# First expert stage with a fixed DRAM region per expert, one tile list after routing, and residual, sum and norm done on the expert tiles

## The reference, cut to what matters

```python
h = h + L2_attn(layernorm(h))   # one head; the diagonal of the scores is masked out
# first experts: top 1 of 8, no capacity limit
x = layernorm(h); route = sigmoid(x @ Wr + br)
e = argmax(route); prob = max(route)
h = h + prob * (gelu(x @ W1[e]) @ W2[e])        # W1 256x1024, W2 1024x256
h = h + L3_attn(layernorm(h))   # 16 heads, causal, with a slope per head
h = h + L3_ffn(layernorm(h))    # second experts, each with a fixed capacity of 333 rows
```

## Time and profile before

| what | us |
|---|---|
| median of 3 runs | 2289.98 (2289.2 to 2295.62) |
| the profiled execution, whole | 2287.08 |
| its span, first to last instruction | 2285.3 |
| PE busy | 1807.9 (79%) |
| DVE busy | 1140.6 (50%) |
| ACT busy | 759.1 (33%) |
| POOL busy | 502.2 (22%) |
| TensorE clock granted, mean | 0.920 of full |

### The profile page before, as it was taken

The page is one execution under the profiler, slowest core; times in us unless marked ns, Lnnn a source line. Parts: engine busy times, 40 slices in busy tenths (PEclk is TensorE's granted clock), DMA queues, the critical chain, the costliest instruction groups (busy, mean ns, idle before and its releaser), DMA issues. The chain is left out here.

```text
span 2285.3 us, 32329 instructions
## 1 busy us (share of the span) xinstructions
PE 1807.9 (79%) x9490; PEld 1178.8 (52%) x9490; DVE 1140.6 (50%) x3699; ACT 759.1 (33%) x1873; POOL 502.2 (22%) x728
## 2 busy tenths in 40 slices
PE   0049999998897989777763999768888888882998
PEld 0024444444665667554541677535666555661676
DVE  5346767673326766744552222156665666641111
ACT  0004444453231245221210221137555566630211
POOL 0130100001101122301111111114434444531122
PEclk9999999998997999899885999859998999995999
DMA  8444544444200000160000101030000010002332
GB/s 179 133 79 89 106 81 87 72 72 121 84 18 0 1 1 1 39 257 12 12 13 24 33 30 33 26 106 9 16 17 19 24 25 19 19 19 59 129 135 70
DMA packets 72299, 129.65 MB, mean 57 GB/s; under 512 B 23030, under 2 KB 59573, under 8 KB 67442
## 3 DMA queue, kind: packets, MB, share of 16 engines
q1 hardware_dynamic: 52636, 107.80, 18.1%
q0 software_dynamic: 17632, 14.26, 2.5%
q10 hardware_dynamic: 1893, 5.99, 0.8%
HBM read 89.79 MB, written 39.52 MB: 57 GB/s over the span
## 5 line engine op out<-in xcount | busy, mean ns | idle before, releaser
L2304 POOL TENSOR_SCALAR l_P<-l_P,l_ri 111x111 f32<-111x111 f32 (+1 forms) x256 | 178.3, 714 | 159.3 <-DVE l_ri L2492 158.4
L653 ACT ACTIVATE PT<-psT 111x666 f32<-111x666 f32 x192 | 139.4, 726 | 156.4 <-PE psT L734 156.0
L2586 ACT ACTIVATE l_P<-l_S,l_nm 111x111 f32<-111x111 f32 (+2 forms) x384 | 179.3, 471 | 32.7 <-DVE l_nm L2485 32.5
L554 DVE TENSOR_REDUCE mx<-psS 111x2 f32<-111x666 f32 x192 | 159.6, 847 | 25.7 <-PE psS L719 25.7
L745 PE MATMUL psO<-PT,vS 111*32 111x333 f32 x768 | 147.0, 461 | 0.1
L2706 PE MATMUL l_psP<-ident,l_P 111*111 111x111 f32 x768 | 108.8, 281 | 32.2 <-DVE l_PT L2501 27.6
L2706 PEld LDWEIGHTS l_psP<-ident,l_P 111*111 111x111 f32 x768 | 95.4, 189 | 62.9 <-issue 33.1
L2042 DVE COPY t_hT<-t_psG 128x512 f32<-128x512 f32 x56 | 36.1, 686 | 175.0 <-PE t_psG L2085 175.0
L2485 DVE CUSTOM_DVE_ANT_0 l_S<-l_psA,l_am 111x111 f32<-111x111 f32 (+1 forms) x256 | 79.0, 331 | 76.9 <-PE l_psA L2692 70.1
L2074 PE MATMUL t_psH<-expert_w,t_xT 128*128 x224 | 103.4, 606 | 1.5 <-DVE t_xT L2035 1.2
L2097 PE MATMUL t_psY<-expert_w,t_hT 128*128 x448 | 101.4, 379 | 0.6 <-ACT t_yb L2007 0.6
(11 more groups left out here) (401 smaller groups left out, 3744.4 us busy)
## 6 DMA issues: line engine op xcount, KB each, us to landing
expert_w<-in_moe_dram SPq DMA_DIRECT2D x8, 2048.0 KB, 24.6
c_w<-in_moe_dram SPq DMA_DIRECT2D x16, 1024.0 KB, 7.2
qs<-halves_scratch SPq DMA_DIRECT2D x128, 83.5 KB, 3.2
ks<-halves_scratch SPq DMA_DIRECT2D x128, 83.5 KB, 4.1
halves_scratch<-high SPq DMA_DIRECT2D x32, 167.0 KB, 3.0
halves_scratch<-low SPq DMA_DIRECT2D x32, 167.0 KB, 3.6
c_xb<-xs_scratch SPq DMA_DIRECT2D x8, 667.3 KB
xs_scratch<-zeros SPq DMA_DIRECT2D x6, 777.0 KB
```

The costliest lines, as they stand in the source:

```text
L554: v.tensor_reduce(mx[J % 2][:, t, c:c + 65:64], psS[s % 2][0:TT, :, 0:T], AX.X, ALU.max, negate=True).then_inc(max_done, 1)
L653: s_.activation(PT[jp % 2][:, :, a, :], psT[0:TT, :, 0:T], ACT.Exp).then_inc(exp_done, 1)
L2304: r = g.tensor_scalar(Pt, Pt, ri[:, c % 2, 2 * t + half:2 * t + half + 1], None, ALU.mult)
L2586: s_.activation(P[c % 4][:, half, at(t):at(t + 1)], Sm[:, half, at(t):at(t + 1)], ACT.Exp, bias=nm[:, c % 2, i:i + 1], scale=-1.0, accum_o ...
```

## The change

It has five parts.

1. `xs` now has a region of 2688 rows for each of the 8 experts, so that a token's row is region start plus rank and `route_place` needs no allocation. `tiles()` builds the list of 28 tiles (their first row in `tile_row`, their expert in `tile_expert`) once, behind the last batch. The zero fill covers 21632 rows of 258 floats, and `xs2` as 2688 rows of 513 floats, all by DMAs of 128 partitions; it is waited for in `quantised`, a stage later.
2. In `masked_attention` the routed rows and slots have two buffers, the order of the pieces is `rl`, `v` 0, `v` 1, `v` 2, `rk`, and `norm(b + 2)` stands between `v` 2 and `rk` in place of `norm(b + 1)` between the first two rows of scores. The add of epsilon is moved to DVE, so POOL's part is one `pow` without a drain. Three whole bodies stand unrolled behind the loop, where there was one.
3. SP writes `h` of each batch to DRAM after attention.
4. In `top1_experts` POOL gathers the residual rows by token to `hb`. DVE multiplies the product by the row's probability (now a column of the row), adds the residual and computes mean and variance; POOL does the `pow`, and DVE writes the normalised row beside the sum. One scatter sends both (2 x 256 floats). ACT no longer copies the product. There are four input buffers, and a tile's load waits for the sum four tiles earlier.
5. `alibi_attention` loads the normalised rows straight to `xn` and all of `h` by one DMA, for which DVE waits ahead of the first scores. `take`, `scale_taken` and `norm` are gone.

```diff
+def stats_and_eps(nc, vector, sh, b):
+    batch_stats(nc, vector, sh, b)
+    return v.tensor_scalar(sh.var_eps[:, :], sh.batch_mv[:, :, 1], EPS, None, ALU.add)
+def eps_scale(nc, sh, b):
+    return nc.gpsimd.tensor_tensor(sh.rs[:, bass.ds(NT * b, NT)], sh.var_eps[:, :], sh.mhalf[0:TT, 0:NT], ALU.pow)
...
 class Fill: write
-            parts = 128 if f.shape[0] % 128 == 0 else TT
-            flat = f.rearrange("(p r) c -> p (r c)", p=parts)
+            flat = f.rearrange("(p r) c -> p (r c)", p=128)
...
 class Routed
-        self.xs = nc.dram_tensor("xs_scratch", [128 * MOE_TILES, ROW1], F32, kind="Internal").ap()
-        self.ys = nc.dram_tensor("ys_scratch", [B * T, D], F32, kind="Internal").ap()
+        self.tile_row = sb("tr", [TT, MOE_TILES], I32)
+        self.xs = dram("xs_scratch", E * REGION + 128, ROW1)
+        self.h = dram("h1_scratch", B * T, D)
+        self.ys = dram("ys_scratch", B * T, 2 * D)
...
 masked_attention, SP and POOL
+            def send(b):
+                sync.wait_ge(stats_done, b + 1)
+                sync.dma_start(routed.h[bass.ds(b * T, T), :].rearrange("(t p) c -> p t c", p=TT),
+                               sh.h[:, bass.ds(NT * b, NT), :]).then_inc(h_sent, 16)
...
             def scale(b):
-                pool.wait_ge(stats_done, b + 1)
+                pool.wait_ge(eps_done, b + 1)
                 pool.sem_inc(begun, 1)
-                batch_scale(nc, pool, sh, sc_tmp, b, "plain", scale_done)
+                eps_scale(nc, sh, b).then_inc(scale_done, 1)
...
 masked_attention, DVE, route_place: 20 instructions of the running allocation out
+                v.tensor_tensor(w[:, :, :], w[:, :, :], oh[:, :, :], ALU.mult)
+                dve.wait_ge(p_ready, b + 1)
+                v.tensor_scalar(pe_m[:, :], pe_m[:, :], 1.0, None, ALU.add)
+                dve.drain()
+                v.tensor_reduce(sl[:, :], w[:, :, :], AX.X, ALU.add)
+                v.reciprocal(row[p][:, :, D + 1], pe_m[:, :])
+                dve.drain()
+                v.tensor_copy(slot[p][:, :], sl[:, :]).then_inc(slot_ready, 1)
+            def tiles():                       # 15 instructions, once
...
                 row_max(0)
-                if not last:
-                    dve.wait_ge(piece_done, base(b))
-                    norm(b + 1)
                 row_max(1)
...
+                piece("rl", 0)
                 piece("v", 0)
-                piece("rl", 0)
                 combine(2)
                 piece("v", 1)
+                piece("v", 2)
+                if later(b):
+                    dve.wait_ge(piece_done, number("x", 1, b, first, last)[1] + 1)
+                    norm(b + 2)
                 piece("rk", 0)
-                piece("v", 2)
                 dve.drain()
-                batch_stats(nc, dve, sh, b).then_inc(stats_done, 1)
+                stats_and_eps(nc, dve, sh, b).then_inc(eps_done, 1)
+                dve.sem_inc(stats_done, 1)
...
 top1_experts, SP
-                if s >= 2:
-                    sync.wait_ge(x_turned, s - 1)
-                    sync.wait_ge(xT_ready, s - 1)
-                sync.dma_start(xb[s % 2][:, :], routed.xs[128 * s:128 * s + 128, :]).then_inc(x_in[s % 2], 16)
+                at = nc.sync.value_load(routed.tile_row[0:1, s:s + 1], min_val=0, max_val=E * REGION)
+                if s >= 4:
+                    sync.wait_ge(y_out, s - 3)
+                sync.dma_start(xb[s % 4][:, :], routed.xs[bass.ds(at, 128), :]).then_inc(x_in[s % 4], 16)
...
 top1_experts, POOL: fetch(s) gathers hb, scale(s) is the pow, send(s) scatters
+            for s in range(NS):
+                if s + 2 < NS:
+                    fetch(s + 2)
                 if s >= 2:
                     send(s - 2)
+                if s >= 1:
+                    scale(s - 1)
...
 top1_experts, DVE
+            def sums(s):
+                dve.wait_ge(y_done, s + 1)
+                dve.wait_ge(hb_in[s % 4], 16 * (s // 4 + 1))
+                if s >= 2:
+                    dve.wait_ge(y_sent[s % 2], 16 * (s // 2))
+                new = yb[s % 2][:, 0:D]
+                v.scalar_tensor_tensor(new, psY[:, 0:D], xb[s % 4][:, D + 1:D + 2], hb[s % 4][:, :], ALU.mult, ALU.add
+                                       ).then_inc(y_out, 1)
+                dve.drain()
+                v.bn_stats(mom[:, :], new)
+                dve.drain()
+                v.bn_aggr(mv[s % 2][:, :], mom[:, :])
+                dve.drain()
+                v.tensor_scalar(ve[s % 2][:, :], mv[s % 2][:, 1:2], EPS, None, ALU.add).then_inc(moments_ready, 1)
+            def rows(s):
+                dve.wait_ge(scaled, s + 1)
+                v.tensor_scalar(yb[s % 2][:, D:2 * D], yb[s % 2][:, 0:D], mv[s % 2][:, 0:1], rs[s % 2][:, 0:1],
+                                ALU.subtract, ALU.mult).then_inc(rows_ready, 1)
...
             for s in range(NS):
                 hidden_out(s)
                 if s + 2 < NS:
                     input_out(s + 2)
+                if s >= 2:
+                    rows(s - 2)
+                if s >= 1:
+                    sums(s - 1)
...
 alibi_attention, SP
-                sync.dma_start(xn[:, :, :], routed.ys[bass.ds(b * T, T), :].rearrange("(t p) c -> p t c", p=TT)
-                               ).then_inc(y_in, 16)
+                sync.dma_start(xn[:, :, :], routed.ys[bass.ds(b * T, T), D:2 * D].rearrange("(t p) c -> p t c", p=TT)
+                               ).then_inc(x_in, 16)
...
             sync.dma_start(br[:, :], ins["c_br"].partition_broadcast(TT)).then_inc(wr_in, 16)
+            sync.dma_start(sh.h[:, :, :], routed.ys[:, 0:D].rearrange("(n p) c -> p n c", p=TT)).then_inc(h_in, 16)
             fetch(1, 2)
             stream.prefetch(sync)
...
 alibi_attention, DVE: take, norm and their calls out; ahead of the first rows()
-            take(1)
+            dve.wait_ge(h_in, 16)
```

More of the change, by code:

```diff
@@ L1186, in dequantise, with quantised @@
         pool.drain()
-def quantised(nc, sh, pre):
+def quantised(nc, sh, pre, fill):
     NS = 3 * B
@@ L1216, in quantised, with _ @@
         tok = lambda banks, t: banks[t // 2][0:TT, D * (t % 2):D * (t % 2) + D]
+        @block.sync
+        def _(sync):
+            fill.wait(sync)
         @block.gpsimd
@@ L1462, in masked_attention @@
         bq = sb("bq", [128, KT])
-        sc_tmp = sb("tmp", [TT, 3, NT])
-        row = sb("row", [TT, NT, ROW1])
+        row = [sb(f"row{i}", [TT, NT, ROW1]) for i in range(2)]
         rT = sb("rT", [128, KT, T])
@@ L1505, in batches, with later @@
             body(0, 0, True, False)
-            with eng.Fori(0, (B - 2) // 2) as i:
+            with eng.Fori(0, (B - 4) // 2) as i:
                 body(2 * i + 1, 1, False, False)
                 body(2 * i + 2, 0, False, False)
-            body(B - 1, 1, False, True)
+            for b in range(B - 3, B):
+                body(b, b % 2, False, b == B - 1)
+        def later(b):
+            return not isinstance(b, int) or b + 2 < B
         def base(b):
@@ L1543, in _ @@
             experts.load(sync, ins["moe1"], range(E))
-            sync.wait_ge(scattered, 16 * NT * B)
+            def send(b):
+                sync.wait_ge(stats_done, b + 1)
+                sync.dma_start(routed.h[bass.ds(b * T, T), :].rearrange("(t p) c -> p t c", p=TT),
+                               sh.h[:, bass.ds(NT * b, NT), :]).then_inc(h_sent, 16)
+            batches(sync, lambda b, p, first, last: send(b))
+            sync.wait_ge(h_sent, 16 * B)
+            for p in range(2):
+                sync.wait_ge(scattered[p], 8 * NT * B)
         @block.gpsimd
@@ L1559, in _ @@
             g.memset(one8[:, :], 1.0)
[L1560 to L1564, removed]
+            for x in (before[:, 0, :], region[:, :]):
+                g.iota(x, pattern=[[REGION, E]], base=0, channel_multiplier=0, allow_small_or_imprecise_dtypes=True)
             pool.drain()
@@ L1690, in route_place @@
-                dve.drain()
-                v.tensor_tensor(past_all[:, :], past_all[:, :], past_now[:, :], ALU.add)
-                dve.drain()
+                v.tensor_copy(routed.tile_row[:, :], used[:, :])
+                v.tensor_copy(routed.tile_expert[:, :], expert[:, :])
             norm(0)
+            dve.wait_ge(piece_done, 2)
+            norm(1)
             for t in range(NT):
@@ L2123 @@
 CAP = B * T // E
+FILL2 = (E * CAP + 127) // 128 * 128
 ROW = 2 * D + 1
@@ L2520, in body @@
                 for c in range(NC):
-                    if c == 0 and not last:
-                        norm(b + 1)
                     if c + 1 < NC or not last:
@@ L2545, in body @@
                         route_rows(b - 1)
-                    if c == 6 and later(b):
-                        take(b + 2)
                 if last:
```

245 lines of the change are left out of this document (114 added, 131 removed).

## The result

The changed kernel takes 2229.99 us (median of 4 runs, 2226.2 to 2233.31), the kernel before 2292.38 in the same session (4 runs, 2289.2 to 2295.62). The ratio is 0.9727, 95% interval 0.9704 to 0.975. Forecast were 2226, range 2209 to 2248.

The account below looks back on a forecast made before the run. Masked attention was taken as bound by a chain crossing engines, neither PE nor DVE full. Terms -32 - 1 - 10 + 0.4 + 0 + 3.6 + 2 - 27 = -64 from 2287.1 gave 2223, with 2.9 for the median 2226; range 2209 to 2248.

Parts of the forecast that it names:

- masked loop, six ends: Masked attention, batch ends 1 to 6: shorter `route_place` and undrained `pow` gain 5.3 us each, -32 in all.
- masked tail, with the register load: End of masked attention: two shorter `route_place` and a `pow` without add and drain, -10; SP's register load from `tile_row`, +0.4.
- first experts, tiles: First experts, 26 tiles: new work and loads are on time, so a tile stays at 7.98 us, 0.
- first experts, the rest: End of first experts: sum, moments, `pow`, row and wakes replace a copy and one wake, +3.6 us.
- alibi head: Ahead of the first alibi scores: the load of `h`, on three engines at 73 GB/s, lands about F + 51 (F: fetch), +2.
- alibi loop: Alibi loop without `take` and `norm`: six times 4.3 us, priced from batch 6 as control, and 1.2 for `norm(1)`, -27.
- zero fill, unchanged stages: Zero fill beside the recurrence, grown from 9.2 to 27.8 MB: ends near 631, hidden, 0.
- P to slot: Masked loop, from `route_place`'s start (P) to the slot's start: from 4.33 to about 1.5 us.
- slot to `pow`: Masked loop, from slot to `pow` start: 9.76 us, of which 3.87 for add and drain goes.
- second rival: First experts held by tile loads or gathers, 0.5 to 0.9 on 26 tiles: +13 to +23, 2239 to 2249; chance 0.11.
- view of 16 engines: Alibi head: were 16 engines used for every DMA, the load of `h` would be fast and the sum 6 us lower.
- first rival: Masked attention: `pow` still waits for POOL's pending scatters, rows 3.9 later in six batches and the tail, 2253; chance 0.07.

Follow-up runs that it names:

- e9: Changed kernel with POOL's add and drain ahead of the `pow` back, and SP's store of `h` held until the next batch's first rows are added; 2265.29 us, one run.
- e2: Changed kernel with 17 small drained DVE instructions added to `route_place`, 11 ahead of the slot's copy and 6 behind; 2265.85 us, ratio 0.9894 to the kernel before.
- e3: Changed kernel with the old order of pieces in masked attention and `norm(b + 1)` again between the first two row maxima; 2229.21 us, ratio 0.9723 to the kernel before.
- c0: Changed kernel run once more, unchanged, as control; 2233.56 us, ratio 0.9741 to the kernel before.
- e5: Changed kernel with the load of `h` in the alibi head split into 96 and 15 partitions; 2231.61 us, ratio 0.974 to the kernel before.
- e7: Changed kernel with the alibi head's load of `h` split into 96 and 15 partitions and masked attention's `pow` ahead of the previous batch's scatters; 2216.25 us.
- e10: Changed kernel with the zero fill written by DMAs of 111 partitions in place of 128, the same 27.8 MB; 2411.73 us, one run.
- e1: Changed kernel with POOL's add of epsilon and the drain behind it put back ahead of the `pow` in masked attention; 2289.01 us, ratio 0.9986 to the kernel before.

## Why the prediction was right, step by step

| step | forecast | measured |
|---|---|---|
| masked loop, six ends | -32 | -35.3 |
| batch 0 and the stage's start | -1 | -1.3 |
| masked tail, with the register load | -9.6 | -8.0 |
| first experts, tiles | 0 | +0.4 |
| first experts, the rest | +3.6 | +4.7 |
| alibi head | +2 | +2.0 |
| alibi loop | -27 | -29.0 |
| zero fill, unchanged stages | 0 | +9.5 |

The forecast had the waits right, and most of their sizes. That the medians come within 4 us of it is in part luck: the loops gained 5.3 more than forecast, the tail and the experts gave 3.1 of that back, and two such executions differ by several us in stages that nothing touches.

**Masked loop.** The terms, from the first two rows of the table of periods: P to slot 2.87 (forecast 2.8), slot to `pow` 4.04 (3.87), given back ahead of P 1.05, the rest 0.1. Net 5.9 a batch for 5.3. The 1.05 is what the forecast's own terms give, 1.65 for `v` 2 and the norm less 0.6 for the norm that left the middle. Its terms sum to 5.6 (6.6 - 1.65 + 0.6), of which it took 5.3.

**What the sum didn't know.** It added the two gains as if each were worth its length. In the changed kernel each is worth more: the drain put back lengthens slot to `pow` by 4.0 and the period by 5.9 (e9), the long `route_place` lengthens P to slot by 2.7 and the period by 5.4 (e2). The surplus is PE's: it is idle for 5.01 and 3.76, its clock falls to half, and the parts of the period behind the rows grow by 1.6 and 2.7. In the kernel before the wait for the `pow` cost PE less, since its last work ahead of the rows ended 13.9 behind P; in e9 that is 8.5. Its rows, and the clock in this idle, still full:

```profile
1188.28 0.54 PE L1890 MATMUL m_psP<-ident,m_P 111*111 111x111 f32 x3 [0.38 <-ACT m_P L1804]
1191.23 0.48 PE L1849 MATMUL m_psM<-ident,m_row 111*128 111x111 f32 x3 [2.40 <-DVE m_row L1612]
```

```profile
1190.00:1191.00 1.00, 0.00 (x0) 0.00 (x0) 1.00 (x5) 0.00 (x0) 0.00 (x0) 1.00 0.00 0
```

Against the kernel before, e9 and e2 gain almost nothing (31.0 to 31.0 and to 30.5), and the changed kernel 5.9. But both have the new order too, which by e3 costs 1.06 ahead of P and gives it back only behind the `pow`. No run has the old order with one wait alone, or the new order with both, so how much of this is the two waits acting together and how much the order stays open. The total was right because both waits went in one change. I read the clock of the whole loop, 0.85, but didn't ask what a shorter wait would do to it.

**Tail.** From the first addition of the last batch to the last slot it is 10.3 shorter, as forecast. From there to the next stage's first load it is 2.3 longer: the stage ends 1.3 later behind its last scatter, and the register load takes 1.0, not 0.4. In c0 this tail took 3.5 more than in the profiled changed kernel, on PE products at half clock (six of them 2.77 there and 1.46 here); so its gain is 4.5 to 8.

**First experts.** The second rival, tile loads or gathers, didn't come: 7.98, with the slack foreseen (1.4, measured 1.25). The end was underestimated by 1: from the last product's end to the next stage 10.7 us against 6.1. The last scatter, twice as wide, is issued by 1442.3 and the stage ends 6.2 later; before it was 3.9. So the chain of sum, moments and row added 2.3 and not 3.6, and the end of the scatter another 2.3 that the forecast didn't have; what it waits for there, no run tells.

**Alibi head.** Three engines at 73 GB/s gave F + 51; it was F + 51.67. By a view of 16 engines the head would have been 6 shorter, and e5, which makes 16 of the 3, measures 4.1 (5.1 in e7). The speed that 16 engines then reach, 200 GB/s and not five times 73, no row of before had told. The Trainium skill, in the section "Why a DMA increments its semaphore by 16 and not by 1" of its page "DMA: Bandwidth & Descriptors", has a DMA of 96 partitions run on 16 engines, and by its rule (the largest number up to 16 that divides) one of 111 on 3. The shares in e5 (1.10), after (0.20) and e10 (0.19) agree.

**Alibi loop.** Batch 6 as a control gave 4.5 less the transpose, 4.3. From c = 6 to the next c = 0 the six batches gained 2.7 to 5.0, 26.1 in all (six times 4.3 is 25.8), and batch 6 nothing. The stage as a whole is less certain than its -29.0: in the ten other executions with this loop unchanged it took 525.4 to 536.8, against 532.75 in the profiled one.

**Zero fill.** The recurrence was 3.9 longer, which looked like its cost. It isn't a fixed one: in ten other executions with the large fill (all but e10) the stage took 169.9 to 174.7, and e2's, at 169.89 and a clock of 0.94, is shorter than the one of before (170.65). Where it took 174.7, the clock was 0.92. Whether the fill makes the lower clock likelier stays open, since only one profile of the kernel before exists. The fill can't be the whole of it: ahead of the recurrence, where the fill hasn't begun and nothing was changed, all twelve executions with the change took 548 to 559 against the 546.00 of that one profile, and the quantised stage took about 159.8 in five of the thirteen executions and 162.4 to 163.0 in the others. So the +9.5 is no term of the change that these runs show.

**The first rival** (the `pow` waits anyway) falls by the timeline after: no idle ahead of it in any of the six batches.

## What to carry over

A wait can cost more than its length: here waits of 2.7 and 4.0 us cost 5.4 and 5.9, as TensorE's clock fell to half while it was idle and its next products were slow. So waits of one batch are best priced together, and with the order that decides what TensorE still has to do meanwhile. An engine that issues indirect DMAs shouldn't drain right behind them, and what others wait for should go ahead of them in its queue. For every DMA of 111 partitions, ask on how many engines it runs: here one such DMA was hidden, one cost 7 us of idle, and a fill of them 180.

## What the runs showed of the hardware that I had not expected

- A drain on POOL behind three indirect scatters lasted until their DMA traffic was over: 3.3 to 4.1 us alone (before, e9), 5.7 to 8.2 with a store of 333 KB on three engines beside them (e1).
- 2.7 MB in rows of 1 KB with a pitch of 2 KB moved at 72 GB/s on 3 engines (24 per engine) and at 200 GB/s on 16 (12.5 per engine), with a share of 1.10. In the zero fill 16 engines moved 416.
- SP was held in the issue of the fill's DMAs until about 21 us (e10), 22 (after) and 29 (before) ahead of the end of their data.
- The same stages of the same code differed between executions by up to 4.8 us (recurrence, 169.9 to 174.7) and by 11 us (the alibi loop, 525.4 to 536.8).
